# Moving one x piece of a GRU step from behind the reset gate into the middle of the update gate

## What is computed

```python
# x: (32, 256, 256), h0 = cond_1024: (32, 256)
Xz = einsum('btc,hc->tbh', x, Wxz) + bxz      # likewise Xr, Xh
for each step:
    Z = sigmoid(xz + H @ Whz.T + bhz)
    R = sigmoid(xr + H @ Whr.T + bhr)
    H_tilda = tanh(xh + R * H @ Whh.T + bhh)  # (R * H) @ Whh.T
    H = Z * H + (1 - Z) * H_tilda
    Y = H @ Whq.T + bhq
out = x + Ys
```

## Time and profile before

| | |
|---|---|
| median of 3 runs | 519.09 us |
| the profiled execution's own time | 519.98 us |
| its span, first to last instruction | 518.2 us |
| mean granted TensorE clock | 0.993 |
| TensorE matmul / weight loads busy | 506.3 us (98%) / 489.4 us (94%) |
| DVE / ACT busy | 307.5 us (59%) / 322.6 us (62%) |
| instructions | 96,066, of which 44,184 matmul records |

### The profile page before, as it was taken

The page is one execution under the profiler, slowest core; times in us unless marked ns, Lnnn a source line. Parts: engine busy times, 40 slices in busy tenths (PEclk is TensorE's granted clock), DMA queues, the critical chain, the costliest instruction groups (busy, mean ns, idle before and its releaser), DMA issues.

```text
span 518.2 us, 96066 instructions
## 1 busy us (share of the span) xinstructions
PE 506.3 (98%) x44184; PEld 489.4 (94%) x44184; DVE 307.5 (59%) x1929; ACT 322.6 (62%) x1800; POOL 0.2 (0%) x4
## 2 busy tenths in 40 slices
PE   8499999999999999999999999999999999999997
PEld 7499999999999999999999999999999999999997
DVE  1256666666666666666666566666666666666665
ACT  2256666666666666666666666666666666666665
POOL 0000000000000000000000000000000000000000
PEclk9889999999999999999999999999999999999999
DMA  5011111111111111111211211211111111111111
GB/s 183 24 47 46 51 55 48 53 51 51 51 51 51 51 51 51 53 49 51 55 46 51 56 46 51 55 48 53 51 50 51 51 51 51 50 51 53 49 51 51
DMA packets 57735, 27.63 MB, mean 53 GB/s; under 512 B 6784, under 2 KB 56832, under 8 KB 57728
## 3 DMA queue, kind: packets, MB, share of 16 engines
q1 hardware_dynamic: 56880, 26.70, 18.5%
q10 hardware_dynamic: 848, 0.83, 0.5%
HBM read 18.98 MB, written 8.52 MB: 53 GB/s over the span
## 4 chain that ended last, share of the span: by engine, by line
PE 96%; issue 2%; DMA 1%; SPq 0%; DVE 0%; ACT 0%; ACTq 0%; DVEq 0%
PE r_ps L253 33%; PE c_ps L253 27%; PE z_ps L253 24%; PE y_ps L253 11%; DMA whq_sb<-in_whq_dram 1%; SPq L117 0%; SPq L119 0%; SPq L118 0%; SPq L115 0%; DVE h_sb L245 0%; DVE o_sb L218 0%; DVE rh_sb L231 0%; DVE u_sb L240 0%; ACT c_ps L193 0%; ACT y_ps L182 0%
## 5 line engine op out<-in xcount | busy, mean ns | idle before, releaser
L253 PE MATMUL c_ps<-xt_sb,wx_sb 128*32 128x64 f32 (+1 forms) x4104 | 174.6, 226 | 1.3 <-issue 1.3
L253 PE MATMUL z_ps<-xt_sb,wx_sb 128*32 128x64 f32 (+1 forms) x4104 | 168.1, 221 | 0.3 <-DMA wx_sb<-in_wx_dram 0.3
L231 DVE TENSOR_TENSOR rh_sb<-y_ps,h_sb 128x32 f32<-128x32 f32 x512 | 89.8, 192 | 126.4 <-ACT y_ps L182 126.4
L182 ACT ACTIVATE y_ps<-r_ps 128x32 f32<-128x32 f32 x512 | 87.3, 182 | 95.5 <-PE r_ps L253 90.1
L253 PE MATMUL z_ps<-h_sb,whz_sb 128*32 128x32 f32 x8192 | 124.3, 198 | 2.1 <-issue 2.1
L253 PE MATMUL c_ps<-rh_sb,whh_sb 128*32 128x32 f32 x8192 | 123.1, 198 | 2.4 <-issue 2.2
L253 PE MATMUL y_ps<-whq_sb,h_sb 128*32 128x128 f32 x2064 | 114.7, 280 | 0.2 <-DVE h_sb L245 0.2
L253 PE MATMUL r_ps<-xt_sb,wx_sb 128*32 128x64 f32 (+1 forms) x4104 | 112.1, 220 | 0.0
L253 PEld LDWEIGHTS z_ps<-h_sb,whz_sb 128*32 128x32 f32 x8192 | 109.1, 111 | 2.3 <-issue 2.3
L253 PEld LDWEIGHTS c_ps<-rh_sb,whh_sb 128*32 128x32 f32 x8192 | 103.5, 110 | 2.6 <-issue 2.3
L253 PEld LDWEIGHTS z_ps<-xt_sb,wx_sb 128*32 128x32 f32 (+1 forms) x4104 | 104.9, 110 | 0.5 <-issue 0.4
(11 more groups left out here) (29 smaller groups left out, 440.0 us busy)
## 6 DMA issues: line engine op xcount, KB each, us to landing
xt_sb<-in_xt_dram SPq DMA_DIRECT2D x130, 64.0 KB, 1.8
xres_sb<-in_xr_dram SPq DMA_DIRECT2D x130, 64.0 KB, 1.8
out_dram<-o_sb SPq DMA_DIRECT2D x130, 64.0 KB, 1.6
wx_sb<-in_wx_dram SPq DMA_DIRECT2D x3, 256.0 KB, 3.1
whr_sb<-in_whr_dram ACTq DMA_DIRECT2D x1, 256.0 KB, 5.1
whz_sb<-in_whz_dram ACTq DMA_DIRECT2D x1, 256.0 KB, 5.8
whh_sb<-in_whh_dram ACTq DMA_DIRECT2D x1, 256.0 KB, 6.0
whq_sb<-in_whq_dram SPq DMA_DIRECT2D x1, 256.0 KB, 6.5
```

The lines of the kernel that those rows point to most:

```text
L182: nc.scalar.activation(r_out[p][o], r_ps[:, o, here], ACT.Sigmoid).then_inc(s_r[o], 1)
L231: nc.vector.tensor_tensor(rh_sb[:, k], r_out[p][k], old[:, k], ALU.mult).then_inc(s_rh[k], 1)
L253: return nc.tensor.matmul(ps, weights, moving, start=start, stop=False, skip_group_check=True, **kw)
```

## The change

N's first x piece (4 matmuls, 8 records) leaves its place between R and the update gate, and stands between the update gate's first output half (`o` = 0, two pieces) and its second (`o` = K - 1 = 1, two pieces). The wait for `s_seed_c` goes with it; the wait for `s_h[1]` (steps with u > 0) stays ahead of the update gate, and so comes directly behind R.

```diff
-                    if s == 0:
-                        pe.wait_ge(s_seed_c, done)
-                    x_piece(q, N, pieces[0])
                     if u > 0:
                         pe.wait_ge(s_h[1], done)
                     for o in range(K):
+                        if o == K - 1:
+                            if s == 0:
+                                pe.wait_ge(s_seed_c, done)
+                            x_piece(q, N, pieces[0])
                         for k in range(K):
                             z_mm = columns(z_ps[p][:, 0], slice(W * o + B * s, W * o + B * s + B), whz_sb, k, o, old[:, k])
                     z_mm.then_inc(s_z_ps, 1)
```

## The result

The changed kernel is slower by 0.6%: 522.67 us (521.27 to 524.0, 8 runs) beside 519.59 us for the one before in the same session (518.16 to 521.44, 8 runs), a ratio of 1.0058 with a 95% interval of 1.0039 to 1.0077. That is 3.0 us. I had forecast 518.5 us, a gain of 0.6 us, so the sign was wrong. The time lies within 1% and in the eight-in-ten range (512.5 to 524.5), but 0.7 us above the forecast's own range of 516 to 522.

A forecast was written before the change was run, and what follows sets the result against it. TensorE's stream, with the recurrence nearly as long beside it, was taken as the bound. 519.98 + 0 (a) - 0.6 (b) + 0 (c) = 519.4; on the runs' median of 519.09 the forecast is 518.5 us, range 516 to 522.

The forecast's parts named there:

- The bound: Loop: TensorE's stream has about 0.05 us of slack per step, the recurrence nearly as long; 64 x 7.72 = 494 us.
- (a): Steps with u > 0: z's first load, waiting for h directly behind R, does not stall; 0, ends 0 and +3.2 us.
- (b): Seeded steps u = 0 and u = 2: N, issued later, no longer loads late behind ACT's seed; -0.6 us.
- (c): Seams between TensorE pieces: as many loads with and without a wait as before; cost 0, bound 3.8 us.
- The paragraph on the change: Update gate: Z's last piece stays behind the same work, so z_sb and zh_sb are due at the same time.
- The slower one: Rival: the wait directly behind R stops TensorE's stream, so z's end and zh come later; 7.7 us, 526.8 us, chance 0.17.
- passes every delay on: zh to the load of r_ps<-zh_sb: zh arrives with nothing to spare, so any delay of z's end reaches that load.
- its two signs: z's first load more than 0.12 us behind h's end; R-to-z longer than before (250.38 to 250.90 on ACT).
- The faster one: Rival: R's second half comes 0.03 us earlier without a 64-column piece directly behind it; 6.4 us, 512.7 us, chance 0.20.
- its observation: R sigmoids start 0.16 us apart for 0.13 of work, tanh 0.09 for 0.065; a 64-column piece follows both second halves.

The follow-up runs named there:

- the first experiment: The kernel before, with only the wait for s_h[1] moved ahead of N's first x piece, directly behind R; N stays in place; ratio 1.0051 (1.0032 to 1.0069).

## Why the prediction was wrong, point by point

**The bound** was read rightly: TensorE's stream and the recurrence are so near to each other that nanoseconds decide, and 64 times an iteration gives the time.

**(a) h's second half loses its cover: 0, right.** The load starts 0.09 us behind h, and the kernel with N after z's first piece shows that the wait behind R is free. The upper end, +3.2 us from the 0.11 us across the branch, was not needed. With N after z's first piece the load starts 75 ns behind h's signal, against 42 for a load that had to wait, so some 35 ns were to spare, as (a) had it.

**(b) N's seed is waited for later: -0.6 us, wrong.** The step of 1.93 instead of 1.91 us was taken as the price of the seed's wait, at least as its bound. It is the output's signal: without that the step is 1.91, and without the seed's wait behind R, in the changed kernel, it keeps its 27 ns over its neighbours (1945 against 1918). N's load is late by some 9 ns in u = 2 of the kernel before (14 ns behind the load ahead of it, 5 in u = 3), as I read it, but with N's seed still waited for behind R and no output signal all three steps are 1912: the lateness costs nothing. The forecast's sign hung on this term alone. Two things differ between that step and the next, and I had looked at one.

**(c) Seams: 0, with a bound of +3.8 us. This is the step that failed.** I wrote that there are "as many seams of each kind as before", and counted pieces and waits only. What the seams do not show is that a signal leaves a delay of 25 ns behind it, which an x piece takes up if it comes within three pieces, and which otherwise reaches Z's end. N's place behind R was the cover of R's first signal, not of h. Measured: 24 ns in the step across the branch, 8 in each of the others, 48 x 64 = 3.1 us; inside the bound of 3.8, but I had taken 0. The forecast's range left this bound out, too: its upper end, +3.2, is that of (a) alone. That the measured 3.1 us is just under that end is luck. The paragraph on the change has the same mistake in other words: z_sb was "due at the same time" because the same pieces stand ahead of it.

**The rivals.** The slower one had the right chain (z's end, ACT, DVE, the load of r_ps<-zh_sb, each with nothing to spare) and the wrong cause; and its claim that zh "passes every delay on" is wrong as well: 26 ns at Z passed on in one step of four. Of its two signs only one came: R to z grew (0.52 to 0.54 us on ACT), but z's load was 0.09 us behind h, not more than 0.12. The faster one did not happen: R's signals stay 159 ns apart whatever stands behind R. But its observation was the clue: of these 159 ns, 16 records at their pace are 134, and the rest is R's first signal. The same holds for the candidate's two signals, 92 ns apart for 67 ns of work. I read the surplus as a matter of what follows, when it was a matter of what had just been signalled.

**What stays open.** Why the starts give way some four pieces behind a signal is not shown, and that this is what sets the limit between three pieces and four is a reading. Nor is it shown by a run of its own how the loss reaches the three steps that do not cross the branch. What the traces have is an order: with the candidate's first matmul at 518 ns (before, and with the spare signal) the step u = 0 is 1910 or 1911, with it at 530 it is 1918, at 534 1923. In the changed kernel the candidate's first signal then comes 3 or 4 ns later, and the next R's 5 more. R's first signal was taken out in one run of each order only, and there with everything behind R later as well; the comparison rests on medians within the two traces.

## What to carry to other kernels

Where TensorE is full of small matmuls, count its signals beside its matmuls: each that nothing covered was some 25 ns here, and one that nobody in the loop needed was worth 0.4% of the kernel (0.3 to 0.6%), against 0.6% for the change under study. A longer piece close behind a signal hides it, so before moving such a piece away, look for the signal that it covers, not only for the wait. And read an experiment by its place in the step before its total: a kernel with the same ratio had its loss in another step, for another reason.

## What the hardware showed that I had not expected

- A matmul's signal lets the matmuls behind it end 23 to 27 ns later (output's: the step from 1937 to 1912 without it; a spare one: Z from 518 to 544), unless an x piece follows closely enough. The Trainium skill (TensorE: Matmul & The Clock Gate, Part 3, The cost: per-tile semaphore tail) gives 26.3 ns for each increment, as a tail of the matmul that raises it. The trace agrees with the size, and shows that matmuls behind it that raise nothing are late by it, too.
- Two semaphores before one TensorE instruction cost 41 ns at Z and 36 in the step (u = 2 of the first experiment), though both had been raised in time; one that was raised in time cost nothing (u = 1 and 3 of the same run).
- A weight load starts 42 ns after the DVE signal for which it waits: rh's two halves and zh are met in this way in the kernel before (42 or 43 ns in every one of the four steps), though TensorE is called busy throughout.
